# Moving the gathers, the inverse roots and two query/key products in a three-stream transformer kernel

## The chip, the cores and the metric

The kernel runs on one core of a Trainium2 chip. The metric is the device time of one launch, in microseconds (us). The engines are called as in the profile: PE (TensorE), DVE (VectorE), ACT (ScalarE), POOL (GpSimd) and SP (SyncE, which issues DMAs).

## The reference

For each of 32 batches of 224 rows of 512 columns, three residual layers follow one another, all in fp32:

```python
x = x + attn(layernorm(x))            # 16 heads of 32 columns, softmax over 224 keys, output product, bias
x = x + xattn(ctx, ctx, layernorm(x)) # one head of 512 columns over 750 context rows
x = x + ffn(layernorm(x))             # router scores over 2048 keys, top 8, softmax w,
                                      # agg = sum_k w_k * aux_values[top_idx_k]
# ffn(h) = h + gate * agg; gate = sigmoid(g1 * u + g0),
# u = clip(0.5 * log1p(var(h)) / mean over all rows of log1p(var(h)) + 2.5 * sigmoid(learned), 0, 5)
```

The gate of any row needs a mean over all rows of all batches, so the gathered sum `agg` of each batch is parked in DRAM and is scaled and added to the output at the very end.

## The kernel before

A batch is held as two tiles of 112 rows (`T` = 2). Its work is cut into steps that belong to streams: N (moments and scaling of the first layer's input), A (self-attention), R (residual load and bias), X (cross-attention), F (router, top 8, uncertainty), G (gather and weighted sum) and Z (the final scaling). One turn `i` of the loop in `pipeline` works on batch i+1 in N, i in A and R, i-1 in X, i-2 in F and i-3 in G. Turns 0 to 2 and 30 and 31 are unrolled, 3 to 29 are a hardware loop, and `LAST` lists what is left after turn 31. `ORDER` is the order of the steps in a turn, written out by hand. Each engine walks through the same list in order and carries out its part of each step, so a step's place in `ORDER` is its place in every engine's queue, and engines meet only by semaphores. `FIRST` and `SETUP` place the weight preparation.

**The attention heads** are done in four groups `k` of four heads. `("A","qk",k)` is the query and key product (24 matmuls, L1145); ACT copies its high part to `qk_hi` (L670) and DVE takes the rest, `qk_lo` (L897), which empties the PSUM bank. `("A","score",k)` is the head-score group, 24 small matmuls (L1211) into the four banks of `psA`; DVE takes the negated maxima `nmax` (L919), ACT exponentiates (L686), DVE normalises in `("A","share",k)` (L932, L934), PE transposes in `("A","prob",k)` (L1154) and ACT copies out (L642), PE mixes with the values in `("A","mix",k)` (L1234), ACT copies `oT_hi` (L703) and DVE takes `oT_lo` (L897). `psA` has four banks, handed out in turn by `FILL`; `scores` waits until all four are empty, among them the one that the step before filled, and the fourth transposed block of `("A","prob",k)` reuses the bank of the mix or product that stands right before it.

**Layer norms.** `statistics` (L828) on DVE: two `bn_stats`, two `bn_aggr`, `ve` = variance + 1e-5 (L840), then the inverse root by a bit-level first guess (L845) and three Newton rounds of three instructions on [112, 2] (L849 to L853), each waiting for the one before. `norm` (L856) then scales the tile. For stream F, `f_norm` does a second round of `bn_stats` and `bn_aggr` on the normed tile (L885, L890) and stores its variance to `var_all` (L893). For stream N the inverse roots go to DRAM (`store_moments`, SP) and come back spread over all partitions (`spread_moments`); DVE multiplies the transposed input with them in `("N","center")` (`centered`, L902).

**The gathers.** A batch needs 16 row gathers, in 8 chunks of two (`gather`, L584 to L593), into a buffer of two chunks, `vg`. POOL issues them as indirect DMAs. `first_gather` issues chunks 0 and 1 after the second top 8, and `next_gather` issues chunk c + 2 as soon as DVE has summed chunk c in `("G","sum",c)` (`g_sum`, L1007), whatever the other engines do at that time. POOL also issues the DMAs that add a bias (`bias_x`, `bias_x1`), adds `x2` and `xnf` in `add_base` (L582), and before any of these waits for eight small loads (`small_loaded`), which ACT issues.

**Around the end of a turn** the list reads `("A","prob",3)`, load, `("G","sum",7)`, `("F","score",3)`, `("F","top",1)`, `("A","mix",3)`, bias; the next turn begins with `("A","qk",0)`, `("A","qk",1)`, `("A","score",0)`.

## Time and profile before

| | |
|---|---|
| median of 3 runs | 2802.99 us (2800.82 to 2810.18) |
| profiled execution, its own time | 2808.96 us |
| its span | 2807.1 us, granted clock 0.971 of full |
| PE busy | 2570.2 us, 92% of the span |
| DVE busy | 2143.4 us, 76% |
| ACT busy | 1438.1 us, 51% |
| POOL busy | 682.9 us, 24% |
| DMA queues, share of 16 engines | 24.3% (issued by POOL) and 23.4% (by SP) |

The page cuts the span into 40 slices; these three lines show PE's busy tenths, DVE's, and the granted clock:

```profile
PE   6899999999999999999999999999999999999830
DVE  5446888888888888888888888888888888887552
PEclk9899999999999999999999999999999999999865
```

PE is busy nine tenths or more in 35 of the 40 slices; the first three and the last three are the preparation of the weights and the final scaling. "issue" as a releaser means that the profile shows nobody that was waited for; "remote" and "another core or an unknown queue" are the same for a wait whose other side has no record.

### The profile page before, as it was taken

The numbers are of one execution on the slowest core, as the hardware profiler recorded it, in microseconds if no ns is written. First come the engines' busy times: TensorE is split into PE (matmuls) and PEld (weight loads), VectorE is DVE, ScalarE is ACT, GpSimd is POOL, SyncE is SP. The second block draws the span as 40 slices with busy tenths as digits, with TensorE's granted clock in tenths as the row PEclk, the third lists the DMA queues.
The fourth block names the chain that finished last, engine by engine and source line by source line (L and its number), as shares of the span: only waits on it lengthen the run. The fifth ranks groups of instructions, "written<-read, shape, count | busy, mean of one in ns | idle before, by whom it ended". The sixth has DMA issues, their size and how long they took to land.

```text
span 2807.1 us, 56939 instructions
## 1 busy us (share of the span) xinstructions
PE 2570.2 (92%) x19090; PEld 2104.5 (75%) x19090; DVE 2143.4 (76%) x4207; ACT 1438.1 (51%) x4247; POOL 682.9 (24%) x650
## 2 busy tenths in 40 slices
PE   6899999999999999999999999999999999999830
PEld 4578878887788788877887888778878887788620
DVE  5446888888888888888888888888888888887552
ACT  2345555555555555555555555555555555555252
POOL 0001222222222222222222222222222222222244
PEclk9899999999999999999999999999999999999865
DMA  5223344454444454544444445444444444443799
GB/s 188 54 78 90 105 128 129 112 137 130 130 129 116 121 130 110 137 130 130 123 114 128 129 113 137 130 130 127 115 123 128 114 137 130 131 122 108 186 209 193
DMA packets 131544, 358.88 MB, mean 128 GB/s; under 512 B 21907, under 2 KB 26515, under 8 KB 123268
## 3 DMA queue, kind: packets, MB, share of 16 engines
q0 software_dynamic: 63520, 160.60, 24.3%
q1 hardware_dynamic: 63190, 192.16, 23.4%
q10 hardware_dynamic: 4784, 5.46, 0.6%
q8 instruction: 30, 0.49, 0.1%
q14 instruction: 20, 0.16, 0.0%
HBM read 316.38 MB, written 41.78 MB: 128 GB/s over the span
## 4 chain that ended last, share of the span: by engine, by line
PE 64%; issue 14%; DVE 10%; ACT 7%; DMA 2%; another core or an unknown queue 1%; POOL 1%; DVEq 0%; POOLq 0%; ACTq 0%; SPq 0%
PE psX L1145 26%; PE psA L1145 19%; PE psA L1211 5%; PE psF L1145 5%; PE psA L1154 4%; ACT pa L686 3%; PE psA L1234 2%; DVE nmax L919 2%; PE psX L1154 2%; DMA vg<-in_L_ffn_aux_values,idx 1%; DVE pa L934 1%; DVE top L1001 1%; DVE idx L1004 1%; ACT xT_hi L665 1%
## 5 line engine op out<-in xcount | busy, mean ns | idle before, releaser
L591 POOL DMA_INDIRECT vg<-in_L_ffn_aux_values,idx x512 | 492.4, 962 | 1585.2 <-DVE agg L1030 1066.8
L686 ACT ACTIVATE pa<-psA,nmax 112x224 f32<-112x224 f32 x1024 | 444.8, 451 | 246.2 <-DVE nmax L919 242.9
L919 DVE TENSOR_REDUCE nmax<-psA 112x4 f32<-112x896 f32 x256 | 267.3, 1086 | 137.1 <-PE psA L1211 125.5
L1145 PE MATMUL psX<-big,gT 128*112 128x375 f32 x1024 | 333.4, 478 | 0.6 <-ACT gT L713 0.6
L1030 DVE SCALAR_TENSOR_TENSOR agg<-vg,wt,agg 112x512 f32<-112x512 f32 x406 | 304.3, 749 | 9.2
L1145 PE MATMUL psX<-pT,cx 125*128 125x224 f32 x1536 | 299.1, 355 | 0.0
L1145 PEld LDWEIGHTS psX<-pT,cx 125*128 125x128 f32 x1536 | 288.0, 190 | 4.0 <-issue 0.3
L934 DVE TENSOR_TENSOR pa<-pa,rsum 112x896 f32<-112x896 f32 x256 | 279.5, 1092 | 8.8
L1145 PEld LDWEIGHTS psX<-big,gT 128*112 128x112 f32 x1024 | 175.2, 176 | 125.9 <-issue 0.9
L1154 PE MATMUL psA<-ident,pa 112*112 112x112 f32 x2048 | 240.6, 263 | 28.4 <-DVE oT_lo L897 24.6
L642 ACT COPY paT<-psA 112x448 f32<-112x448 f32 x512 | 243.3, 555 | 21.5 <-PE psA L1154 16.9
L1154 PEld LDWEIGHTS psA<-ident,pa 112*112 112x112 f32 x2048 | 202.1, 134 | 63.9 <-DVE oT_lo L897 38.1
L686 ACT ACTIVATION_READ_ACCUMULATOR pa<-psA,nmax 112x1 f32 x1024 | 212.1, 207 | 0.0
L1145 PE MATMUL psX<-xnxT,m 128*128 128x224 f32 x1024 | 201.8, 356 | 0.6 <-ACT xnxT L642 0.6
L1145 PEld LDWEIGHTS psX<-xnxT,m 128*128 128x128 f32 x1024 | 193.1, 192 | 1.4 <-ACT xnxT L642 1.0
L723 ACT ACTIVATE nx<-psX,xmax 112x375 f32<-112x375 f32 x128 | 72.4, 571 | 225.3 <-issue 161.0
L1001 DVE MAX8 top<-sc 112x8 f32<-112x2048 f32 x64 | 146.5, 2290 | 35.0 <-ACT sc L642 35.0
L1145 PE MATMUL psA<-xT_hi,wqT_hi 128*128 128x224 f32 x512 | 153.4, 300 | 5.9 <-DVE wkT_lo L1052 5.9
L642 ACT COPY sc<-psF 112x512 f32<-112x512 f32 x256 | 138.1, 594 | 19.2 <-PE psF L1145 17.4
L670 ACT CAST qk_hi<-psA 128x448 fp32r<-128x448 f32 x128 | 68.3, 533 | 154.0 <-PE psA L1145 154.0
L1004 DVE FIND_INDEX8 idx<-top,sc 112x8 uint32<-112x2048 f32 x64 | 146.3, 2286 | 0.0
L1145 PE MATMUL psA<-wvT_hi,xT_hi 128*112 128x256 f32 x512 | 143.7, 281 | 0.0
(220 smaller groups left out, 5952.9 us busy)
## 6 DMA issues: line engine op xcount, KB each, us to landing
big<-in_ctx_t SPq DMA_DIRECT2D x32, 1500.0 KB, 7.9
cx<-in_ctx SPq DMA_DIRECT2D x32, 1344.0 KB
xa<-in_x SPq DMA_DIRECT2D x64, 224.0 KB
centered<-in_x_t SPq DMA_DIRECT2D x32, 448.0 KB, 4.7
x<-in_L_attn_bff POOLq DMA_DIRECT2D x32, 448.0 KB, 6.2
x<-cb_scratch POOLq DMA_DIRECT2D x32, 448.0 KB, 5.9
x<-in_x SPq DMA_DIRECT2D x31, 448.0 KB
out<-x SPq DMA_DIRECT2D x30, 448.0 KB, 3.1
```

The costliest lines, as they stand in the source:

```text
L591: pool.indirect_dma_start(vg[:, c % SLOTS, k, :], None, aux_values, bass.IndirectOffsetOnAxis(ap=idx[:, t, n:n + 1], axis=0))\
L642: nc.scalar.copy(dst, src).then_inc(drained[s][j % banks[s]], 1)
L686: last = nc.scalar.activation(pa[:, t, h, :], psA[0:R, h, t * S:(t + 1) * S], ACT.Exp, bias=nmax[:, k % 2, h, t:t + 1], accum_out=rsum[:, ...
L723: nc.scalar.activation(px[:, t, j * HK:(j + 1) * HK], bank("X", job)[0:R, 0:HK], ACT.Exp, bias=xmax[:, t:t + 1], accum_out=xsum[:, t, j:j ...
L919: nc.vector.tensor_reduce(nmax[:, k % 2, h:h + 2, :], psA[0:R, h:h + 2, 0:T * S].rearrange("p h (t s) -> p h t s", t=T), AX_X, ALU.max, ne ...
L934: nc.vector.tensor_tensor(pa[:, t, :, :], pa[:, t, :, :], rsum[:, k, t, :].unsqueeze(2).to_broadcast([R, HB, S]), ALU.mult).then_inc(a_sha ...
L1001: mark("F", nc.vector.max(top[:, t, :], sc[0:R, :]))
L1004: nc.vector.max_index(idx[:, t, :], top[:, t, :], sc[0:R, :]).then_inc(sc_searched, 1)
L1030: last = nc.vector.scalar_tensor_tensor(dst, vg[:, c % SLOTS, k, :], w, dst, ALU.mult, ALU.add)
L1145: last = nc.tensor.matmul(dst, stationary, moving, start=n == 0, stop=n == len(pairs) - 1)
L1154: return nc.tensor.transpose(dst, src, ident[0:k, 0:k])
L1211: last = nc.tensor.matmul(psA[0:R, h, t * S:(t + 1) * S], qkT[q][own, k % 2, t * R:(t + 1) * R], qkT[key][own, k % 2, S:2 * S], start=n == ...
```

## The change

- `("G","sum",c)` no longer issues gathers. New steps `("G","gather",p)` and `("F","gather",0)` issue chunks 2p and 2p+1, four indirect DMAs in a row (`behind_scores`). In the loop POOL first waits until the head-score group before it in the list is complete. The sums of chunks 0 and 1 move into the turn before, as `("F","sum",0)` and `("F","sum",1)`, one on either side of `("A","mix",3)`.
- The inverse root of all three norms becomes one POOL instruction, `ve ** -0.5`, in new steps `("N"/"X"/"F","root",0)`. `statistics` keeps its first three steps and stands in a `"stat"` step of its own; for N it moves from behind `("A","score",1)` to behind `("A","score",0)`.
- The second statistics of stream F go. POOL computes variance times inverse root squared, by two instructions behind `add_base`, and stores them to `var_all`; ACT's final logarithm waits for that.
- `("A","qk",0)` and `("A","qk",1)` of batch i+1 become `("Q","qk",0)` and `("Q","qk",1)` in turn i, between `("A","prob",3)` and `("A","mix",3)`.
- `("F","score",3)` moves up between the two `("X","out")` steps, `("G","sum",7)` behind `("A","score",3)`, `("X","prob",0)` in front of `("A","mix",0)`, `("X","prob",1)` behind `("A","mix",1)`, and value and the third query/key product change places. `("X","enter")` becomes two steps, one for each tile. `LAST` is rewritten to match.

```diff
 ORDER = (
-    ("A", "qk", 0), ("A", "qk", 1), ("A", "score", 0), ("G", "sum", 0), ("A", "share", 0), ("X", "enter", 0),
-    ("X", "norm", 0), ("A", "value", 0), ("G", "sum", 1), ("A", "qk", 2), ("X", "turn", 0), ("A", "prob", 0),
-    ("F", "norm", 0), ("X", "query", 0), ("A", "score", 1), ("N", "norm", 0), ("F", "turn", 0), ("X", "score", 0),
-    ("N", "spread", 0), ("G", "sum", 2), ("G", "sum", 3), ("A", "qk", 3), ("A", "share", 1), ("X", "score", 1),
-    ("N", "center", 0), ("F", "route", 0), ("A", "mix", 0), ("X", "prob", 0), ("A", "prob", 1), ("F", "learn", 0),
-    ("X", "prob", 1), ("G", "sum", 4), ("F", "score", 0), ("A", "mix", 1), ("F", "score", 1), ("G", "sum", 5),
-    ("A", "score", 2), ("F", "top", 0), ("A", "share", 2), ("G", "sum", 6), ("X", "mix", 0), ("X", "mix", 1),
-    ("A", "prob", 2), ("F", "score", 2), ("A", "score", 3), ("X", "out", 0), ("A", "share", 3), ("X", "out", 1),
-    ("A", "mix", 2), ("A", "prob", 3), ("R", "load", 0), ("G", "sum", 7), ("F", "score", 3), ("F", "top", 1),
-    ("A", "mix", 3), ("R", "bias", 0),
+    ("A", "score", 0), ("N", "stat", 0), ("A", "share", 0), ("X", "enter", 0), ("X", "enter", 1), ("A", "qk", 2),
+    ("G", "gather", 1), ("N", "root", 0), ("X", "stat", 0), ("X", "root", 0), ("X", "norm", 0), ("A", "value", 0),
+    ("N", "spread", 0), ("X", "turn", 0), ("F", "stat", 0), ("G", "sum", 2), ("A", "prob", 0), ("F", "root", 0),
+    ("F", "norm", 0), ("X", "query", 0), ("G", "sum", 3), ("A", "score", 1), ("G", "gather", 2), ("F", "turn", 0),
+    ("A", "share", 1), ("X", "score", 0), ("A", "qk", 3), ("G", "sum", 4), ("X", "score", 1), ("N", "center", 0),
+    ("F", "route", 0), ("X", "prob", 0), ("A", "mix", 0), ("A", "prob", 1), ("F", "learn", 0), ("F", "score", 0),
+    ("G", "sum", 5), ("A", "mix", 1), ("X", "prob", 1), ("F", "score", 1), ("A", "score", 2), ("F", "top", 0),
+    ("G", "gather", 3), ("A", "share", 2), ("X", "mix", 0), ("X", "mix", 1), ("G", "sum", 6), ("A", "prob", 2),
+    ("F", "score", 2), ("A", "score", 3), ("G", "sum", 7), ("X", "out", 0), ("F", "score", 3), ("A", "share", 3),
+    ("X", "out", 1), ("A", "mix", 2), ("A", "prob", 3), ("F", "top", 1), ("F", "gather", 0), ("Q", "qk", 0),
+    ("R", "load", 0), ("F", "sum", 0), ("Q", "qk", 1), ("A", "mix", 3), ("R", "bias", 0), ("F", "sum", 1),
 )
...
-FIRST = (("N", "norm", 0), ("N", "spread", 0), ("W", "mean", 0), ("N", "center", 0), ("W", "split", 0),
+FIRST = (("N", "stat", 0), ("N", "root", 0), ("N", "spread", 0), ("W", "mean", 0), ("N", "center", 0), ("W", "split", 0),
          ("W", "mean", 1), ("W", "mean", 2), ("W", "split", 1), ("W", "split", 2), ("W", "keys", 0),
-         ("W", "keys", 1),)
+         ("W", "keys", 1), ("Q", "qk", 0), ("Q", "qk", 1), ("W", "keys", 2))
...
             def store_moments(b, _):
-                sp.wait_ge(steps["N"], N_STEPS * (b + 1))
+                sp.wait_ge(rooted["N"], b + 1)
...
                 nc.gpsimd.tensor_tensor(dst[:, :, :], x2[:, :, :], xnf[:, :, :], ALU.add).then_inc(base_ready, 1)
+                nc.gpsimd.tensor_tensor(var_part[:, :], mv["F"][:, :, 1], rstd["F"][:, :], ALU.mult).then_inc(var_step, 1)
+                pool.wait_ge(var_step, b + 1)
+                nc.gpsimd.tensor_tensor(columns(var_all, b), var_part[:, :], rstd["F"][:, :], ALU.mult).then_inc(var_taken, 1)
+
+            def norm_root(s):
+                def step(b, _):
+                    pool.wait_ge(steps[s], per_batch[s] * b + MOMENTS)
+                    if s == "N":
+                        wait(pool, moments_stored, 16 * b)
+                    apart(pool)
+                    nc.gpsimd.tensor_tensor(rstd[s][:, :], ve[s][:, :], power[:, :], ALU.pow).then_inc(rooted[s], 1)
+                return step
...
-            def next_gather(b, c):
-                if c + SLOTS < CHUNKS:
-                    gather(b, c + SLOTS)
-
-            def first_gather(b, t):
-                if t == 1:
-                    for c in range(SLOTS):
-                        gather(b, c)
+            def behind_scores(b, pair):
+
+                if not (isinstance(b, int) and b + 3 >= B + (pair == 0)):
+                    k = (pair - 1) % NB
+                    for h in range(HB):
+                        wait_full(pool, "A", head_job(k, h), b + 3 - (pair == 0))
+                for c in range(SLOTS * pair, SLOTS * pair + SLOTS):
+                    gather(b, c)
...
             def norm(s, b, src, dst, normed):
-                statistics(s, b, src, rstd[s][:, :])
+                dve.wait_ge(rooted[s], b + 1)
```

## Rows read from the trace of the kernel before

**Rows 1.** Windows: us, busy of PE, PEld, DVE, ACT, POOL (instructions), clock, DMA, GB/s

```profile
1000.00:2000.00 1000.00, 970.18 (x7394) 805.32 (x7393) 820.67 (x1629) 534.24 (x1611) 253.17 (x237) 1.00 0.46 125
```

**Rows 2.** Waits of PE, 1000 to 2000 us: engine, line, waited for: total, times, longest

```profile
PE psA L1211 <- issue: 18.6, 13, 1.4
...
PE psA L1154 <- DVE oT_lo L897: 8.4, 25, 0.4
```

**Rows 3.** PE timeline, two turns of the loop: start, us, line, out<-in [idle<-releaser]

```profile
1250.61 0.36 PE L1211 MATMUL psA<-qk_hi 32*112 32x224 f32 x4 [1.43 <-issue]
...
1265.39 0.93 PE L1154 MATMUL psX<-ident,nx 112*128 112x112 f32 x8
...
1294.71 0.59 PE L1154 MATMUL psA<-ident,pa 112*112 112x112 f32 x4 [0.39 <-DVE oT_lo L897]
...
1312.18 0.36 PE L1211 MATMUL psA<-qk_hi 32*112 32x224 f32 x4
...
1331.31 0.36 PE L1211 MATMUL psA<-qk_hi 32*112 32x224 f32 x4 [1.43 <-issue]
...
1392.85 0.36 PE L1211 MATMUL psA<-qk_hi 32*112 32x224 f32 x4
...
1411.31 0.36 PE L1211 MATMUL psA<-qk_hi 32*112 32x224 f32 x4 [1.43 <-issue]
```

**Rows 4.** DVE timeline, the same turns, columns as in PE's

```profile
1251.59 2.09 DVE L919 TENSOR_REDUCE nmax<-psA 112x4 f32<-112x896 f32 x2 [1.18 <-PE psA L1211]
...
1261.11 0.17 DVE L840 TENSOR_SCALAR ve_X<-mv_X 112x2 f32<-112x2 f32 x1
...
1294.27 0.39 DVE L897 TENSOR_TENSOR oT_lo<-psA,oT_hi 128x224 fp32r<-128x224 f32 x1
...
1314.64 2.09 DVE L919 TENSOR_REDUCE nmax<-psA 112x4 f32<-112x896 f32 x2 [1.91 <-remote]
...
1330.47 0.62 DVE L897 TENSOR_TENSOR qk_lo<-psA,qk_hi 128x448 fp32r<-128x448 f32 x1 [0.68 <-ACT qk_hi L670]
...
1394.65 2.09 DVE L919 TENSOR_REDUCE nmax<-psA 112x4 f32<-112x896 f32 x2 [1.25 <-PE psA L1211]
```

**Rows 5.** POOL timeline, the gathers beside head-score group 3, columns as in PE's

```profile
1313.73 0.92 POOL L591 DMA_INDIRECT vg<-in_L_ffn_aux_values,idx  x1 [0.30 <-issue]
...
1394.40 0.93 POOL L591 DMA_INDIRECT vg<-in_L_ffn_aux_values,idx  x1 [0.30 <-issue]
```

**Rows 6.** Waits of all engines, whole run, columns as in PE's waits

```profile
DVE nmax L919 <- remote: 11.6, 6, 1.9
```

**Rows 7.** Groups by line on DVE: out<-in xcount | busy us, mean ns | idle

```profile
L1030 DVE SCALAR_TENSOR_TENSOR agg<-vg,wt,agg 112x512 f32<-112x512 f32 x406 | 304.3, 749 | 9.2
...
L849 DVE SCALAR_TENSOR_TENSOR tmp_X<-rstd_X,ve_X 112x2 f32<-112x2 f32 x96 | 15.5, 161 | 4.1 <-DVE rstd_X L853 0.3
```

**Rows 8.** ACT timeline, around the first mix and the loop's end, columns as in PE's

```profile
1293.82 0.34 ACT L703 CAST oT_hi<-psA 128x224 fp32r<-128x224 f32 x1
...
1294.05 0.45 ACT L642 COPY pT<-psX 125x336 f32<-125x336 f32 x1
...
1329.91 0.53 ACT L670 CAST qk_hi<-psA 128x448 fp32r<-128x448 f32 x1 [2.03 <-PE psA L1145]
```

**Rows 9.** Groups by line on POOL, columns as in those of DVE

```profile
L582 POOL TENSOR_TENSOR x<-x,nx 112x1024 f32<-112x1024 f32 x31 | 73.0, 2355 | 93.5 <-DVE nx L859 93.5
```

**Rows 10.** DVE timeline, first 90 us: the first batch's scaled input

```profile
25.72 1.09 DVE L902 TENSOR_TENSOR centered<-centered,spread 128x896 f32<-128x896 f32 x1 [12.69 <-DMA spread<-moments_scratch]
```

**Rows 11.** ACT timeline, first 90 us: the last of the eight small loads

```profile
23.48 0.45 ACTq L619 DMA_DIRECT2D gbc<-in_L_ffn_gate_bias  x1
```

**Rows 12.** DMA issues, first 60 us: queue, size, us to landing

```profile
gbc<-in_L_ffn_gate_bias ACTq DMA_DIRECT2D x1, 0.4 KB, 3.7
```

**Rows 13.** PE timeline, end of the first batch's head mix

```profile
92.94 1.00 PE L1154 MATMUL psA<-ident,pa 112*112 112x112 f32 x4 [3.67 <-DVE oT_lo L897]
```

**Rows 14.** Windows, first batch, columns as in the first group

```profile
90.00:100.00 10.00, 5.31 (x46) 3.14 (x47) 5.06 (x9) 3.86 (x8) 0.00 (x0) 0.60 0.44 155
```

More of the change, by code:

```diff
@@ L28 @@
 F32R = mybir.dt.float32r
-I32 = mybir.dt.int32
 U32 = mybir.dt.uint32
@@ L231, in build @@
         rstd = {s: sb(f"rstd_{s}", [R, T]) for s in "NXF"}
-        tmp = {s: sb(f"tmp_{s}", [R, T]) for s in "NXF"}
+        power = sb("power", [R, T])
+        var_part = sb("var_part", [R, T])
         var_all = sb("var_all", [R, B * T])
@@ L540, in _ @@
                           ("W", "cb"): first_cxT, ("W", "gb"): first_ctx,
-                          ("X", "score"): next_cxT, ("X", "mix"): next_ctx, ("N", "norm"): store_moments,
+                          ("X", "score"): next_cxT, ("X", "mix"): next_ctx, ("N", "root"): store_moments,
                           ("N", "spread"): spread_moments, ("N", "center"): next_xt, ("X", "enter"): entered, ("R", "load"): next_xr,
                           ("F", "norm"): store_base,
-                          ("G", "sum"): store_agg})
+                          ("G", "sum"): store_agg, ("F", "sum"): store_agg})
             for k in range(LATE + B - DIRECT):
@@ L558, in _ @@
             nc.gpsimd.memset(one[:, :], 1.0)
+            nc.gpsimd.memset(power[:, :], -0.5).then_inc(const_step, 1)
+            pool.wait_ge(const_step, 2)
             nc.gpsimd.memset(rwT[:, RD:LO], 0.0)
@@ L612, in _ @@
             pool.wait_ge(small_loaded, 16 * SMALL)
-            pipeline(pool, {("Z", "scale"): add_scaled,  ("R", "bias"): bias_x, ("X", "norm"): bias_x1, ("F", "norm"): add_base,
-                            ("G", "sum"): next_gather, ("F", "top"): first_gather})
+            pipeline(pool, {("Z", "scale"): add_scaled,  ("R", "bias"): bias_x, ("N", "root"): norm_root("N"), ("X", "root"): norm_root("X"), ("F", "root"): norm_root("F"), ("X", "norm"): bias_x1, ("F", "norm"): add_base,
+                            ("G", "gather"): behind_scores, ("F", "gather"): behind_scores})
         @block.scalar
@@ L835, in statistics @@
                 apart(dve)
+                if s == "F":
+                    wait(dve, var_taken, b)
+                    apart(dve)
                 for t in range(T):
@@ L937, in share, with x_enter @@
                 assert k < NB - 1 or count["A"] == A_STEPS
[L939 to L945 removed]
+            def x_enter(b, t):
+                if t == 0:
+                    dve.wait_ge(xr_biased, 16 * (b + 1))
+                j = FILL["X", "enter", t]
+                wait_full(dve, "X", j, b)
+                nc.vector.tensor_tensor(x1[:, t, :], bank("X", j)[0:R, :], x1[:, t, :], ALU.add)\
+                    .then_inc(drained["X"][j % banks["X"]], 1)
             def x_maxima(b, t):
```

102 lines of the change are left out of this document (39 added, 63 removed), and 68 rows, old and new, of tables (LAST, SETUP).

## The prediction

> **What bounds the kernel now.** I read the windows first: between 1000 and 2000 us PE is busy 970.18 of 1000 us at full granted clock, DVE 820.67 [rows 1]. So PE bounds the loop, and an edit pays there only as far as it takes away one of PE's gaps, about 2.4 us in a turn of 80. The waits of PE name them [rows 2]: 18.6 us in 13 waits in front of a head-score group, 8.4 us in 25 in front of the fourth transposed block of a `prob` step. The PE timeline places them [rows 3]. The first is 1.43 us, in front of head-score group 0 at 1250.61, 1331.31 and 1411.31: PE has run out of work and waits for the second query/key product to be copied by ACT and DVE. The blocks cost 0.39 us at 1294.71 (head group 1) and, by what is left of the 8.4 us over 12.4 turns, 0.29 us in head group 3. The turns are not equal: 1250.61 to 1331.31 is 80.70 us, 1331.31 to 1411.31 is 80.00. From head-score group 3 to the next turn's group 0 they take 19.13 us (1312.18 to 1331.31) and 18.46 us (1392.85 to 1411.31), so the whole difference arises there.
>
> **Why there:** the maxima on DVE. Behind head-score group 0 they begin 0.98 us after the group (1250.61, 1251.59). Behind group 3 they begin after 1.80 us (1392.85, 1394.65) or after 2.46 us (1312.18, 1314.64), and DVE sits idle meanwhile, 1.25 or 1.91 us [rows 3, 4]. POOL is issuing gathers at that moment: the second of a pair begins at 1394.40, 0.25 us before the maxima of the quicker turn; in the slower one it begins at 1313.73 and ends at 1314.65, when the maxima begin [rows 5]. I read this as: a gather that is being issued while a head-score group ends holds back the news of that end by 0.8 or 1.5 us. The longer delay is the "remote" wait, 6 in the whole run [rows 6], so I take 6 turns in 28 for slow ones, 0.22.
>
> **The change, part by part,** first a turn of the loop.
>
> *Gathers behind a head-score group.* POOL now waits until the group is complete, as DVE does, and four gathers take about 5 us, so none is running when the next group ends. The maxima of group 3 then come at 0.98. Behind them the chain of DVE from the maxima to `qk_lo` took 16.45 us in the slow turn (1314.64 to 1331.09 [rows 4]). It loses some 2 us of waiting and gains the chunk sum that now stands in front of the second `qk_lo`, two instructions and two small ones, some 1.9 us at 0.75 an instruction [rows 7]. So it ends near 0.98 + 16.4 = 17.4 us, and PE is the later one:
>
> *Query/key products moved back.* The wait of 1.43 us does not vanish, it changes its object: group 0 needs all four banks, and `("A","mix",3)` now fills the last of them, directly in front of it. In place of `qk_hi` (0.53) and `qk_lo` (0.62) the wait covers `oT_hi` (0.34) and `oT_lo` (0.39) [rows 4, 8]: 1.43 - 0.19 - 0.23 = 1.01 us. Queued behind it is all of PE. With `("F","score",3)` moved up as cover, the 0.29 us of head group 3 go too. Head-score group 3 to the next group 0: 18.46 - 1.43 - 0.29 + 1.01 = 17.75 us. That is 0.71 less in a normal turn and 1.38 less in a slow one, 0.78 x 0.71 + 0.22 x 1.38 = 0.86 us in the mean.
>
> *X prob 0 in front of mix 0.* ACT now copies `pT` before `oT_hi`. In the trace `oT_hi` stands at 1293.82, `oT_lo` at 1294.27, the block at 1294.71 [rows 3, 4, 8]. `oT_hi` moves to about 1294.15 and `oT_lo` behind DVE's own copy of that step, to about 1294.70, so the block waits till 1295.14. PE's work up to it is the same, hence 0.43 us more of waiting. X prob 1 behind mix 1 covers later banks that had no wait; nothing.
>
> *Roots on POOL.* Per turn DVE loses 27 Newton instructions at 161 ns [rows 7], three first guesses and the second statistics, some 7 us. PE never waits for these in the loop, so this is worth nothing there. What counts is the way back. X norm waits for POOL, and behind it in DVE's queue stand X norm, F stat and the sums; PE's X turn waits for it. Before, `ve_X` is ready 10.67 us and X turn due 14.78 us after group 0 [rows 3, 4]. After, N stat (1.9) stands in front, the Newton rounds are gone, both enters and the third `qk_lo` come first; I add DVE's queue up to `ve_X` at 12.3 us. The norm takes 1.0, so a root may take 14.8 - 13.3 = 1.4 us from `ve_X` to DVE's next start. The trace has no small two-input instruction on POOL. Upper end: the [112, 1024] addition, 2.36 us [rows 9], and 0.7 of signalling, 3.1 us. Lower end: 0.3, signalling alone. I take 0.7, near the lower end, since a root has 2 columns and the addition 1024. That hides. N root has 25 us until it is needed, F root has a chunk sum beside it, and SP's spread of the moments comes earlier.
>
> The Trainium skill (GPSIMD Engine Reference, 3.1) gives 4497 ns for an addition of 2048 columns; with the 2355 ns of this trace for 1024 [rows 9] that leaves an estimate of 0.2 us for two. By it the root takes about 0.5 us, and the sum stays.
>
> A turn: -0.86 + 0.43 = -0.43 us; 28 turns: **-12 us**. Bounds: -1.0 (the 0.43 doesn't come) to +0.3 a turn (the delay isn't the gathers').
>
> *Start.* DVE had the first root ready at 13.0 us and then waited 12.69 us for its store and spread, while the weights were loading; the input is scaled at 25.72 [rows 10]. Now the root is POOL's, and POOL waits for eight small loads before its first step. The last is issued at 23.48 and lands 3.7 us later, at 27.2 [rows 11, 12]; the root comes near 27.8, and store and spread follow. With the queues emptier I take 7.7 us, so the input is scaled at 35.5: **+9.8 us** (7 to 14), and nothing hides it, since the splits of the weights stand behind it in DVE's queue.
>
> *First turns.* The second batch's moments come 25 us earlier, so the spread is there when DVE asks. PE's wait of 3.67 us [rows 13] goes, and with it most of the half clock behind it (0.60 granted from 90 to 100 us, that is, near 1.2 GHz [rows 14]): **-7 us** (-3.7 to -9). Turns 1 and 2 have the same gaps and some more at `prob` and `mix`: **-2 us**.
>
> *Tail.* Before X turn of the last batch DVE drops nine Newton instructions and a first guess (about 2 us with their gaps), and a chunk sum leaves from in front of it (1.3), against 0.7 for the root and, later, 0.5 for the variance behind `add_base`: **-2.2 us** (-8 to +6), if the scaling that follows starts so much earlier.
>
> Sum: 9.8 - 7 - 2 - 12 - 2.2 = **-13.4 us**. The profiled execution took 2808.96 us, 1.9 more than its span, and becomes 2795.6. It lies 6 us above the median, so on the median: 2802.99 - 13.4 = **2789.6 us**.
>
> **The rivals.**
> *Late root (slower).* If POOL needs more than 1.4 us for the way `ve_X`, root, DVE, PE waits for X turn in each of 30 turns. For: a power is no addition, and no row prices it. Against: two columns only. At 2.2 us: 0.8 x 30 = 24 us, 2813.6; at the upper end of 3.1: +51, 2841. It outweighs the gain from 1.4 + 13.4/30 = 1.85 us on. Chance 0.13.
> The skill's same page (2.1) says that the first call of freshly loaded POOL code costs about 6 us; paid once, in the start, where the first root is on the path, it would give 2795.6, and no row here shows it.
> *Late gathers (slower).* Chunk 0 is now issued behind group 3 and summed in front of the second `qk_lo` and of `oT_lo`, both of which PE waits for. It has some 7 us to land, beside the context load, as the chunks of group 3 had before, when DVE did not wait. Decides from 7 us on; 1 us late is +28, 2818. Chance 0.07.
> *The delay is not the gathers'* or follows them to where they now run (mix 2). The 0.6 to 0.9 us of the loop stay, the 0.43 comes: 2789.6 + 12 = 2802. For: two clock readings side by side are no cause. Chance 0.22.
> *No growth at the first mix,* so -25 us, 2777.6. Chance 0.08.
>
> **How the numbers follow.** Forecast 0.50 (2781 to 2797). The range takes in "no growth" and most of the late rivals: 2773 to 2814. A measurement of this kernel tells 0.3%, 8.4 us, from no change. Faster by more (below 2794.6): 0.46 of the forecast's 0.50, the 0.08 of the last rival and 0.04 of the third, together 0.58. Within: the other 0.04 of the forecast and 0.18 of the third, 0.22. Slower (above 2811.4): the first two rivals, 0.20.
>
> **What the profile after would show.** The maxima of groups 2 and 3 begin 1.0 us after their group; no "remote" waits. Group 3 to group 0 takes 17.75 us, with a wait of 1.0 in front of group 0 that `oT_lo` ends. The block at mix 0 waits 0.8. X turn has no wait, and the root lasts below 1 us. The first scaled input stands near 35.5. DVE's busy time falls by some 220 us. A wait at X turn, or of DVE for `vg`, would make the prediction wrong.

## The result, and the profile after

| | before | after |
|---|---|---|
| median, us | 2804.19 (2800.82 to 2810.18, 4 runs) | 2768.00 (2767.13 to 2768.09, 4 runs) |
| ratio, 95% interval | | 0.9873 [0.9857, 0.9889] |
| profiled execution, us (its span) | 2808.96 (2807.1) | 2767.93 (2766.1) |
| DVE busy, us | 2143.4 | 1976.6 |
| turn of the loop, mean of 28, us | 80.19 | 79.11 |

The changed kernel is faster by 36 us, 1.3%. I had forecast 13 (2789.6, range 2773 to 2814): the sign is right, the size is not.

The start of head-score group 0 in turns 1, 3 and 31 cuts the 41.0 us by which the spans of the two profiled executions differ into stages (before's execution lies 4.8 us above the median of its four, so the medians differ by 36.2 only). With the forecast beside them:

| stage | before | after | difference | forecast |
|---|---|---|---|---|
| to group 0 of turn 1 | 132.06 | 129.93 | -2.1 | +2.8 |
| turns 1 and 2 | 156.03 | 155.86 | -0.2 | -2 |
| turns 3 to 30 | 2245.42 | 2215.06 | **-30.4** | -12 |
| from there to the end | 273.59 | 265.25 | -8.3 | -2.2 |

The page of after, its first part: busy time, share, instructions.

```profile
PE 2549.4 (92%) x19090; PEld 2107.2 (76%) x19090; DVE 1976.6 (71%) x3087; ACT 1442.4 (52%) x4247; POOL 862.9 (31%) x811
```

The window that answers to [rows 1], columns as there:

```profile
1000.00:2000.00 1000.00, 976.54 (x7468) 816.60 (x7467) 763.63 (x1197) 549.52 (x1645) 330.44 (x305) 1.00 0.48 126
```

PE is still the bound and idles 1.9 us a turn in place of 2.4. Its waits over the whole run (those of [rows 2] are of one stretch), columns as there:

```profile
PE psA L1216 <- DVE oT_lo L902: 32.7, 31, 1.1
PE psA L1159 <- DVE oT_lo L902: 24.9, 30, 0.9
```

One turn of its timeline, columns as in [rows 3]:

```profile
1314.24 0.36 PE L1216 MATMUL psA<-qk_hi 32*112 32x224 f32 x4 [1.05 <-DVE oT_lo L902]
...
1328.92 0.93 PE L1159 MATMUL psX<-ident,nx 112*128 112x112 f32 x8
...
1358.63 0.59 PE L1159 MATMUL psA<-ident,pa 112*112 112x112 f32 x4 [0.82 <-DVE oT_lo L902]
...
1363.19 0.36 PE L1216 MATMUL psA<-qk_hi 32*112 32x224 f32 x4
...
1375.75 0.36 PE L1216 MATMUL psA<-qk_hi 32*112 32x224 f32 x4
...
1393.37 0.36 PE L1216 MATMUL psA<-qk_hi 32*112 32x224 f32 x4 [1.10 <-DVE oT_lo L902]
```

The wait before group 0 is 1.05 to 1.10 us and ended by `oT_lo` (forecast 1.01; it was 1.43 [rows 3]). The block at the first mix waits 0.82 (forecast 0.8). X turn at 1328.92 has no wait. DVE's timeline of the same turn:

```profile
1326.36 0.17 DVE L863 TENSOR_SCALAR ve_X<-mv_X 112x2 f32<-112x2 f32 x1
1327.51 1.00 DVE L869 TENSOR_SCALAR nx<-x,mv_X,rstd_X 112x512 f32<-112x512 f32 x2 [0.98 <-POOL rstd_X L603]
...
1332.89 3.51 DVE L1035 SCALAR_TENSOR_TENSOR agg<-vg,wt,agg 112x512 f32<-112x512 f32 x2
...
1364.19 1.09 DVE L924 TENSOR_REDUCE nmax<-psA 112x4 f32<-112x896 f32 x1 [1.31 <-PE psA L1216]
...
1376.75 1.09 DVE L924 TENSOR_REDUCE nmax<-psA 112x4 f32<-112x896 f32 x1 [0.73 <-PE psA L1216]
```

POOL's:

```profile
1326.71 0.69 POOL L603 TENSOR_TENSOR rstd_X<-ve_X,power 112x2 f32<-112x2 f32 x1 [4.33 <-DVE ve_X L863]
...
1333.06 2.80 POOL L592 TENSOR_TENSOR x<-x,nx 112x1024 f32<-112x1024 f32 x1 [1.22 <-DVE nx L869]
...
1365.22 0.92 POOL L613 DMA_INDIRECT vg<-in_L_ffn_aux_values,idx  x1 [19.78 <-issue]
...
1377.84 0.92 POOL L613 DMA_INDIRECT vg<-in_L_ffn_aux_values,idx  x1 [8.01 <-issue]
```

The gathers now begin 2.0 and 2.1 us after groups 2 and 3 (1363.19, 1375.75), the maxima 1.00 us after them, where they came after 1.8 and 2.5 at group 3 [rows 3, 4]. No "remote" wait is left and no turn is longer than the others: the turns take 79.08 to 79.16 us, the last 79.30. The root lasts 0.69 us.

### The profile page after: what moved, and what is told of

The parts are those of the page before. It is cut to its first block, busy times and chain, and to the rows that moved or that the text cites. A ratio compares the mean times of both kernels' runs of the same rounds, so it can differ in the third digit from the quotient of the medians.

```text
span 2766.1 us, 55689 instructions
## 1 busy us (share of the span) xinstructions
PE 2549.4 (92%) x19090; PEld 2107.2 (76%) x19090; DVE 1976.6 (71%) x3087; ACT 1442.4 (52%) x4247; POOL 862.9 (31%) x811
## 4 chain that ended last, share of the span: by engine, by line
PE 78%; DVE 8%; ACT 5%; issue 4%; DMA 2%; POOL 1%; ACTq 1%; DVEq 0%; POOLq 0%
PE psX L1150 41%; PE psA L1150 17%; PE psA L1159 6%; PE psF L1150 5%; PE psA L1216 4%; PE psA L1239 3%; PE psX L1159 2%; ACT L769 1%; DMA vg<-in_L_ffn_aux_values,idx 1%; DVE xmax L955 1%; PE psF L1159 1%; DVE top L1006 1%; ACT xT_hi L687 1%; DVE oT_lo L902 1%; DVE idx L1009 1%
## 5 line engine op out<-in xcount | busy, mean ns | idle before, releaser
L613 POOL DMA_INDIRECT vg<-in_L_ffn_aux_values,idx x512 | 542.8, 1060 | 1208.1 <-issue 1071.3
L1035 DVE SCALAR_TENSOR_TENSOR agg<-vg,wt,agg 112x512 f32<-112x512 f32 x406 | 361.6, 891 | 10.7
L1159 PE MATMUL psA<-ident,pa 112*112 112x112 f32 x2048 | 229.4, 263 | 24.9 <-DVE oT_lo L902 24.9
L1159 PEld LDWEIGHTS psA<-ident,pa 112*112 112x112 f32 x2048 | 202.0, 134 | 57.2 <-DVE oT_lo L902 31.5
L664 ACT COPY paT<-psA 112x448 f32<-112x448 f32 x512 | 237.6, 553 | 14.9 <-PE psA L1159 14.6
L902 DVE TENSOR_TENSOR qk_lo<-psA,qk_hi 128x448 fp32r<-128x448 f32 x128 | 79.2, 619 | 112.5 <-ACT qk_hi L692 112.3
```

Of the source, the lines that this page charges most:

```text
L613: pool.indirect_dma_start(vg[:, c % SLOTS, k, :], None, aux_values, bass.IndirectOffsetOnAxis(ap=idx[:, t, n:n + 1], axis=0))\
L664: nc.scalar.copy(dst, src).then_inc(drained[s][j % banks[s]], 1)
L902: return nc.vector.tensor_tensor(dst, src, hi.bitcast(F32), ALU.subtract)
L1035: last = nc.vector.scalar_tensor_tensor(dst, vg[:, c % SLOTS, k, :], w, dst, ALU.mult, ALU.add)
L1159: return nc.tensor.transpose(dst, src, ident[0:k, 0:k])
```

## Experiments

All kernels of a series ran on one chip (the first two series on the same one), each compared with the kernel before beside it. Group starts below are from PE's timelines, "lag" is the time from a head-score group's start to its maxima on DVE. Mean spacing of the groups over turns 3 to 30, us:

| kernel | group 0 to 1 | 1 to 2 | 2 to 3 | 3 to 0 | turn |
|---|---|---|---|---|---|
| before | 23.25 | 25.44 | 12.88 | 18.61 | 80.19 |
| e1, before with gathers behind groups 2, 3 | 23.23 | 25.46 | 12.56 | 18.01 | 79.27 |
| after | 23.16 | 25.81 | 12.56 | 17.58 | 79.11 |
| e2, after, gathers free | 23.52 | 26.80 | 13.33 | 17.59 | 81.25 |
| e3, after, X prob 0 behind mix 0 | 23.19 | 25.41 | 12.56 | 17.58 | 78.74 |
| e5, before with a clock on ACT; no lags | 23.27 | 25.43 | 12.56 | 17.99 | 79.26 |
| e6, after, Newton on DVE | 25.30 | 25.80 | 12.57 | 17.60 | 81.27 |
| e7, after, qk 0 and 1 in their own turn | 23.23 | 25.81 | 12.57 | 18.88 | 80.49 |
| e8, after, F score 3 behind prob 3 | 25.05 | 25.81 | 12.57 | 19.63 | 83.05 |
| e12, after, root twice | 23.71 | 25.81 | 12.56 | 17.58 | 79.66 |
| e15, e2's kernel again; no lags | 23.17 | 25.80 | 12.57 | 17.59 | 79.13 |

**First series: the gathers, the swap, the first root.** The kernel before took 2805.05 us (2799.11 to 2806.99, 7 runs).

e1 is the kernel before with GpSimd waiting until group 2 or 3 is complete (`behind`); no step moves:

```diff
             def next_gather(b, c):
+                if c == 4:
+                    behind(2, b + 3)
...
                 if t == 1:
+                    behind(3, b + 2)
                     for c in range(SLOTS):
```

> The kernel before, with one edit: GpSimd waits for head-score group 2 before it issues the four gathers that ran beside it, and for group 3 before the first two of the next pair. Nothing else moves. Theory (a gather issued while a group ends holds the maxima back, and late maxima of group 2 are also what makes PE wait inside the third prob step): the maxima of groups 2 and 3 begin 1.0 us after their group, no turn is longer than the others, group 2 to group 3 falls from 12.86 to 12.56 us; a turn falls from 80.19 in the mean to 79.7, the time by 10 to 14 us, ratio 0.995. My prediction's own step knew only the slow turns here: 4 us. Rival (the delay is not the gathers', it comes from the sums on DVE): lags stay 1.7 to 1.8, ratio 1.000.

Measured 2777.89 us, ratio 0.9905 [0.9889, 0.9922]: 27 us, twice what even the better theory gave, and three quarters of the whole change. A turn loses 0.92 us in two places. The first is the third `prob` step. In before, on PE, and then DVE's second `share`:

```profile
1389.98 2.02 PE L1154 MATMUL psA<-ident,pa 112*112 112x112 f32 x16
1391.77 0.46 PE L1145 MATMUL psF<-rk,rq_hi 113*112 113x512 f32 x1
```

On DVE:

```profile
1389.80 1.09 DVE L934 TENSOR_TENSOR pa<-pa,rsum 112x896 f32<-112x896 f32 x1
```

The same steps in e1, on PE, and on DVE also the maxima of group 3, which stands at 1378.27 there (lag 1.01):

```profile
1375.70 1.70 PE L1162 MATMUL psA<-ident,pa 112*112 112x112 f32 x16
1377.17 0.47 PE L1153 MATMUL psF<-rk,rq_hi 113*112 113x512 f32 x1
```

On DVE:

```profile
1374.89 1.09 DVE L942 TENSOR_TENSOR pa<-pa,rsum 112x896 f32<-112x896 f32 x1
...
1379.28 1.09 DVE L927 TENSOR_REDUCE nmax<-psA 112x4 f32<-112x896 f32 x1 [0.78 <-PE psA L1219]
```

Sixteen transposed blocks take 1.79 us up to the next step in before and 1.47 in e1. The timeline groups them in one row, so no wait is printed, but the second `share` ends at 1390.89 in before, when eight of the blocks (0.75 us) are through and the other eight need it; in e1 it ends at 1375.98, 0.28 us after the step began. That is 0.32 us a turn, from group 2's maxima. The other place is the fourth `prob` step, on PE in before:

```profile
1401.91 0.59 PE L1154 MATMUL psA<-ident,pa 112*112 112x112 f32 x4 [0.26 <-DVE oT_lo L897]
1402.28 0.46 PE L1145 MATMUL psF<-rk,rq_hi 113*112 113x512 f32 x1
```

And in e1:

```profile
1385.74 1.75 PE L1162 MATMUL psA<-ident,pa 112*112 112x112 f32 x16
1387.25 0.46 PE L1153 MATMUL psF<-rk,rq_hi 113*112 113x512 f32 x1
```

The step began at 1400.30 in before: 1.98 us against 1.51 in e1, with no step moved. The `oT_lo` it waits for stood in DVE's queue behind the late maxima. With the turns of 0.67 us more, group 3 to group 0 loses 0.60 in the mean.

e2 takes the waits out of the changed kernel:

```diff
             def behind_scores(b, pair):
-                if not (isinstance(b, int) and b + 3 >= B + (pair == 0)):
-                    k = (pair - 1) % NB
-                    for h in range(HB):
-                        wait_full(pool, "A", head_job(k, h), b + 3 - (pair == 0))
                 for c in range(SLOTS * pair, SLOTS * pair + SLOTS):
```

> The changed kernel without the waits for the head-score groups in front of the fours; the gathers keep their place in GpSimd's order and go as soon as their slots are free, so by the sums' times some run at about 23, 48 and 61 us of a turn, where groups 1, 2 and 3 end. Theory: maxima lag by 1.5 to 1.9 us where a gather is beside the end of a group, the third prob step again takes 1.7 to 1.8 us in place of 1.47, a turn grows from 79.11 by 0.3 to 0.6 us: ratio to the kernel before 0.990 to 0.994, +8 to +17 us on the changed kernel. Rival (the gain has nothing to do with the gathers): 0.987 as the changed kernel.

Measured 2831.88 us, ratio 1.0093 [1.0076, 1.0110]: 64 us more than the changed kernel. Lags of 1.9 or 2.6, 2.4 and 2.2 us at groups 0, 1 and 2; at group 3, where no gather is beside, 1.0. The direction is as expected, the size four times the upper end.

e3 puts `("X", "prob", 0)` behind `("A", "mix", 0)` again:

```diff
-    ("F", "route", 0), ("X", "prob", 0), ("A", "mix", 0), ("A", "prob", 1),
+    ("F", "route", 0), ("A", "mix", 0), ("X", "prob", 0), ("A", "prob", 1),
```

> The changed kernel with X prob 0 put behind A mix 0 again, as before the change. Theory (ACT's pT copy ahead of oT_hi costs PE 0.43 us in each turn): the wait in front of the fourth block of head group 1 falls from 0.82 to 0.4 us, group 1 to group 2 from 25.80 to 25.4, a turn from 79.11 to 78.7, the time by 11 to 12 us to about 2756: ratio 0.983. Rival (what PE gains there it waits for at the next X step or at head-score group 2): a turn stays 79.1, ratio 0.987.

Measured 2755.95 us, ratio 0.9829 [0.9813, 0.9846]: 12 us. A row of PE's waits shows it; it was 24.9 in 30:

```profile
PE psA L1159 <- DVE oT_lo L902: 12.2, 31, 0.7
```

e4 moves one line:

```diff
                     nc.gpsimd.tensor_tensor(rstd[s][:, :], ve[s][:, :], power[:, :], ALU.pow).then_inc(rooted[s], 1)
+                    if s == "N" and isinstance(b, int) and b == 0:
+                        pool.wait_ge(small_loaded, 16 * SMALL)
...
-            pool.wait_ge(small_loaded, 16 * SMALL)
             pipeline(pool, {
```

> The changed kernel with GpSimd's wait for the eight small loads moved behind its first root. Theory (that wait alone delayed the first scaled input): root at 10.8 instead of 24.3 us, its store and spread under the weight loads as before the change, first scaled input near 25 us instead of 33.1, score group 0 near 48.5 instead of 56.1, the time 7 to 8 us shorter, near 2760: ratio 0.9845. Rival (the load queues set it, and what is gained is waited for at the weights or at the first turn's set-up work): 0 to 3 us, ratio 0.987.

Measured 2765.46 us (2760.08 to 2766.94), ratio 0.9864 [0.9848, 0.9880]. On POOL and on DVE:

```profile
11.26 0.73 POOL L603 TENSOR_TENSOR rstd_N<-ve_N,power 112x2 f32<-112x2 f32 x1 [8.84 <-DVE ve_N L864]
```

On DVE:

```profile
26.30 1.09 DVE L908 TENSOR_TENSOR centered<-centered,spread 128x896 f32<-128x896 f32 x1 [15.23 <-DMA spread<-moments_scratch]
```

The same steps in the changed kernel, on POOL:

```profile
24.30 0.73 POOL L603 TENSOR_TENSOR rstd_N<-ve_N,power 112x2 f32<-112x2 f32 x1 [21.89 <-DMA gbc<-in_L_ffn_gate_bias]
```

On DVE:

```profile
33.09 1.09 DVE L907 TENSOR_TENSOR centered<-centered,spread 128x896 f32<-128x896 f32 x1 [22.29 <-DMA spread<-moments_scratch]
```

The root comes 13.0 us earlier, the scaled input 6.8: store and spread take 14.3 us beside the weight loads and 8.1 behind them. In the profiled execution group 0 of turn 1 stands 6.3 us earlier and the end 7.9; the median of four gains 2.5. The mechanism is as expected, its worth varies between executions.

**Second series: what the other edits are worth.** Here the kernel before took 2777.18 us (2775.09 to 2778.87, 7 runs), 28 less than before. e5 shows why: it is the kernel before with a clock on ACT.

```diff
+                if k == 3:
+                    wait_full(act, "A", head_job(k, 3), b)
+                    nc.scalar.copy(probe[:, :], one[:, :])
```

> The kernel before; ACT also waits for head 3 of head-score group 3 and copies one column of a constant then, as a clock of when the news of the group reaches another engine (in that place ACT is idle for 2.2 us). If PE's signal itself is held up by a gather, the copy stands 1.7 to 1.8 us after the group, as the maxima do. If only DVE is held up, the copy stands at 1.0 us or less and the maxima still at 1.8. No change in time, 2800 to 2810 us.

Measured 2779.72 us, in one execution. ACT, DVE and POOL around group 3 at 1376.88:

```profile
1377.93 0.19 ACT L685 COPY probe<-one 112x1 f32<-112x1 f32 x1 [0.18 <-PE psA L1215]
```

On DVE:

```profile
1377.88 2.09 DVE L923 TENSOR_REDUCE nmax<-psA 112x4 f32<-112x896 f32 x2 [0.74 <-PE psA L1215]
```

On POOL:

```profile
1376.91 0.92 POOL L592 DMA_INDIRECT vg<-in_L_ffn_aux_values,idx  x1 [7.66 <-DVE agg L1034]
```

A gather runs from 0.03 to 0.95 us after the group, and the maxima come at 1.00. At group 2 the gather runs from 0.27 to 1.24 us and the maxima come at 1.15; in the profiled execution of before it ran from 0.26 to 1.25 there, and they came at 1.74. A turn takes 79.26 us: that of e1, 79.27, and each of the four spacings is e1's within 0.04 us. So in this series gathers beside a group's end cost nothing, and late maxima cost the kernel before the same 0.9 us a turn whether their absence comes by e1's edit or by itself. The copy on ACT, 1.05 us behind the group's start (the texts of e13 and e17 put it at 0.8), could not say which engine is late, since none was.

e6 takes all three roots back to DVE, Newton's rounds as before the change, in the new order:

```diff
                 mark(s, nc.vector.tensor_scalar(ve[s][:, :], mv[s][:, :, 1], EPS, None, ALU.add))
+                mark(s, nc.vector.tensor_scalar(root.bitcast(I32), ve[s][:, :].bitcast(I32), -0.5, RSQRT_SEED,
+                                                ALU.mult, ALU.add))
+                for _ in range(3):
...
             def norm(s, b, src, dst, normed):
-                dve.wait_ge(rooted[s], b + 1)
```

> The changed kernel with all three roots back on DVE by Newton's rounds, in the new order of steps. Theory: N's and X's rounds (2.1 us each) stand in DVE's queue before nx, GpSimd's way of 1.15 us goes; nx begins 2 to 3 us later than 13.27 us into the turn, PE waits 1.5 to 2.5 us for X turn in each turn, +40 to +70 us; the start gains back the 7.4 us, the tail loses 3 to 4: 2800 to 2835 us, ratio 1.000 to 1.011. Rival (DVE's queue has room, the roots are worth nothing in the loop as my prediction said): no wait at X turn, the time about 2764, ratio 0.986.

Measured 2827.56 us, 60 above the changed kernel's 2768. PE and DVE:

```profile
1355.95 0.51 PE L1175 MATMUL psX<-ident,nx 112*128 112x112 f32 x3 [1.70 <-DVE nx L885]
```

On DVE:

```profile
1354.81 1.00 DVE L885 TENSOR_SCALAR nx<-x,mv_X,rstd_X 112x512 f32<-112x512 f32 x2 [0.15 <-DVE rstd_X L880]
```

`nx` begins 15.46 us into the turn in place of 13.27, and X turn 16.60 in place of 14.68. In three of the 28 turns group 0 to 1 takes 26.98 us in place of 25.11; in the first of them the granted clock is 0.60 from 381.24 to 384.24 us, behind PE's wait for `nx`. In the old order the same rounds cost PE nothing [rows 3]; in the new one GpSimd's roots are what makes room.

e7 puts the two products back at the head of their turn, and takes them out of the steps ahead of the loop:

```diff
-    ("A", "score", 0), ("N", "stat", 0),
+    ("A", "qk", 0), ("A", "qk", 1), ("A", "score", 0), ("N", "stat", 0),
...
-    ("F", "gather", 0), ("Q", "qk", 0), ("R", "load", 0), ("F", "sum", 0), ("Q", "qk", 1), ("A", "mix", 3),
+    ("F", "gather", 0), ("R", "load", 0), ("F", "sum", 0), ("A", "mix", 3),
...
-         ("W", "keys", 1), ("Q", "qk", 0), ("Q", "qk", 1), ("W", "keys", 2))
+         ("W", "keys", 1), ("W", "keys", 2))
```

> The changed kernel with the first two query/key products back at the head of the next turn. Theory: the wait in front of group 0 covers qk_hi and qk_lo again, 1.43 in place of 1.05 to 1.10 us: +0.35 a turn, +10 to +12 us, ratio 0.991. Rival (the wait is set by the sum in front of qk_lo on DVE, whatever the order): no change, 0.987, or more than 1 us a turn.

Measured 2831.47 us. Group 3 to group 0 grows by 1.30 us, not 0.35: prob 3 and mix 3 now stand directly behind one another (PE waits 0.77 for `paT`), and the wait before group 0 is 1.47. Another 23 us are lost before turn 1 (152.67 against 129.93). `SETUP` counts the A steps of the first turn, so with two more of them at its head every later piece of weight preparation also comes two A steps earlier; how the 23 us divide between that and the products is not shown. The rival's "more than 1 us a turn" is nearer than the theory.

e8 puts F score 3 back:

```diff
-    ("X", "out", 0), ("F", "score", 3), ("A", "share", 3), ("X", "out", 1), ("A", "mix", 2), ("A", "prob", 3), ("F", "top", 1),
+    ("X", "out", 0), ("A", "share", 3), ("X", "out", 1), ("A", "mix", 2), ("A", "prob", 3), ("F", "score", 3), ("F", "top", 1),
```

> The changed kernel with F score 3 back behind prob 3. By my prediction's step (it is only cover for one block): the block waits 0.3 us again, +8 us, ratio 0.990. Theory now: DVE's search for the top eight follows it by 2.1 us, and behind the search stand both qk_lo, a sum and oT_lo, so group 0 starts about 2.2 us later in each turn: +60 us, ratio 1.008 to 1.010, with a wait of some 3 us in front of group 0 that oT_lo ends.

Measured 2885.20 us: 117 above the changed kernel, of which group 3 to 0 gives 2.05 us a turn, close to the 2.2, and group 0 to 1 another 1.9 that nobody expected. PE and DVE:

```profile
1451.88 0.53 PE L1216 MATMUL psA<-qk_hi 32*112 32x224 f32 x4 [2.65 <-DVE oT_lo L902]
```

On DVE:

```profile
1443.77 2.29 DVE L1006 MAX8 top<-sc 112x8 f32<-112x2048 f32 x1 [2.37 <-ACT sc L664]
```

The search begins at 74.45 us of its turn in place of 70.75. The 1.9 us are no wait: `nx` is late in the turn, but PE does not wait at X turn. They are TensorE's clock. PE has idled 2.65 us in front of group 0, and the window behind it, columns as in [rows 1], has a granted clock of 0.50, that is, near 1.2 GHz:

```profile
1451.80:1456.30 4.50, 4.42 (x31) 3.50 (x32) 4.20 (x6) 1.70 (x7) 1.40 (x2) 0.50 0.01 2
```

The same stretch of the changed kernel, behind a wait of 1.10 us:

```profile
1393.30:1397.80 4.50, 4.43 (x40) 3.52 (x41) 4.46 (x6) 2.06 (x9) 1.97 (x2) 1.00 0.54 91
```

Some of the matmuls behind group 0 take 0.63 us in place of 0.40, in all 28 turns. So of the 117 us some 57 are the later search (28 times 2.05) and some 53 come through the clock (28 times 1.89).

**Third series: both together, and the changed kernel once more.** The kernel before took 2804.38 us (2802.31 to 2809.11, 7 runs). e9 has the edits of e3 and e4, shown there:

> The changed kernel with both edits that paid alone: X prob 0 behind A mix 0 (12 us) and GpSimd's wait for the small loads behind its first root (2.5 to 8 us). They lie in different stages and add: 2748 to 2754 us. Its gathers stand behind the head-score groups, so the time should be the same whether the kernel before takes 2805 us (ratio 0.981) or 2777 us (0.991) beside it.

Measured 2747.18 us (2744.76 to 2749.49), ratio 0.9794 [0.9777, 0.9810]. This version beats both kernels.

e10 is the changed kernel with no edit:

> The changed kernel, unchanged, timed beside the kernel before once more, since the kernel before took 2805 us in the first series and 2777 in the second, without any late maxima in the second. Theory (the delay by gathers is a property of where or when the kernel runs; the changed kernel has no gather beside the end of a group and so never shows it): the changed kernel takes 2766 to 2770 us either way; ratio 0.987 if the kernel before takes 2805, 0.997 if it takes 2777. Rival (everything gets faster by 1 percent in the second series): 2740 us beside 2777, ratio 0.987.

Measured 2768.66 us, ratio 0.9873 [0.9856, 0.9889], as the first time. It was never timed in a series without lags; e6, e7 and e8 are set against 2768 from elsewhere, but the spacings that they leave alone are the changed kernel's within 0.07 us (table).

e11 is e2's kernel, with e2's edit:

> The changed kernel without the waits in front of the fours, as in e2 (there 2832 us, 64 us above the changed kernel, with lags of 1.6 to 2.6 us at groups 0, 1 and 2). Theory: where the kernel before takes 2777 us a gather beside the end of a group delays nothing; lags 1.0 to 1.2, the time within 6 us of the changed kernel. Where the kernel before takes 2805 it is again near 2832.

Measured 2829.04 us, ratio 1.0089 [1.0071, 1.0107], with e2's lags, and 60 us above e10 beside it.

e12 computes each root twice:

```diff
+                    nc.gpsimd.tensor_tensor(spare_root[s][:, :], ve[s][:, :], power[:, :], ALU.pow).then_inc(root_step[s], 1)
+                    pool.wait_ge(root_step[s], b + 1)
                     nc.gpsimd.tensor_tensor(rstd[s][:, :], ve[s][:, :], power[:, :], ALU.pow).then_inc(rooted[s], 1)
```

> The changed kernel with each root on GpSimd computed twice, one after the other, the first into a spare tile. The way from ve_X to nx grows from 1.15 by 0.7 to 0.9 us. X turn is due 14.68 us into the turn and nx ends at 14.27; by Newton on DVE nx came 2.19 later and X turn 1.92, so the slack is 0.27 us: PE waits 0.45 to 0.6 us for X turn in each turn, +13 to +18 us: 2781 to 2786. By my prediction's limit (1.4 us from the end of ve_X, measured 0.98): +0.3 to 0.5 a turn, +8 to +14.

Measured 2786.61 us (2783.19 to 2790.71), 18 above the changed kernel.

```profile
1338.88 0.79 PE L1163 MATMUL psX<-ident,nx 112*128 112x112 f32 x6 [0.32 <-DVE nx L873]
```

On DVE:

```profile
1337.74 1.00 DVE L873 TENSOR_SCALAR nx<-x,mv_X,rstd_X 112x512 f32<-112x512 f32 x2 [1.74 <-POOL rstd_X L607]
```

`ve_X` to `nx` takes 1.91 us in place of 1.15, and a turn 0.55 more. So 0.2 us of 0.76 were slack.

**Fourth to sixth series: the lag itself.** The kernel before took 2778.66, 2778.03 and 2779.36 us here. None of the traces of e13 to e18 shows a lag, so all but e15 answer nothing they were made for.

> The changed kernel without the waits in front of the fours. Beside a kernel before at 2804 us: 2829 to 2832 as twice measured. Beside one at 2777 us: lags of 1.0 to 1.2 us with gathers beside the ends of groups 0, 1 and 2, and 2766 to 2775 us.

e15, e2's kernel a third time, measured 2769.47 us (2765.77 to 2771.52), ratio 0.9965 [0.9953, 0.9977]: the time of the changed kernel, and 60 us less than twice before. The same group 1 in e11, on PE:

```profile
1363.50 0.36 PE L1212 MATMUL psA<-qk_hi 32*112 32x224 f32 x4
```

On POOL:

```profile
1363.73 1.05 POOL L613 DMA_INDIRECT vg<-in_L_ffn_aux_values,idx  x1 [0.75 <-issue]
```

On DVE:

```profile
1365.93 1.09 DVE L920 TENSOR_REDUCE nmax<-psA 112x4 f32<-112x896 f32 x1 [3.38 <-PE psA L1212]
```

And in e15, on PE:

```profile
1340.04 0.36 PE L1212 MATMUL psA<-qk_hi 32*112 32x224 f32 x4
```

On POOL:

```profile
1340.23 1.05 POOL L613 DMA_INDIRECT vg<-in_L_ffn_aux_values,idx  x1 [0.75 <-issue]
```

On DVE:

```profile
1341.05 2.09 DVE L920 TENSOR_REDUCE nmax<-psA 112x4 f32<-112x896 f32 x2 [2.00 <-PE psA L1212]
```

The gather lies at 0.23 to 1.28 us behind the group in one, at 0.19 to 1.24 in the other; the maxima come at 2.43 and at 1.01. Set beside each other, the two traces differ, in the median, in no other wait of DVE or ACT for PE: `xmax`, for one, starts 0.58 us after the start of its last matmul in both.

> As e5: the kernel before with ACT's one-column copy when head 3 of head-score group 3 is done. Where the kernel before takes 2804 us: if PE's signal is late, the copy stands at 1.7 us or more behind the group (2.4 in the slow turns); if only DVE is held up, at 0.8 to 1.0 with the maxima at 1.8 to 2.5. Where it takes 2777 us: 0.8 us as in e5, and the maxima at 1.0.

e14 is e1 without its wait for group 3:

```diff
                 if t == 1:
-                    behind(3, b + 2)
                     for c in range(SLOTS):
```

> The kernel before with the four gathers beside group 2 moved behind that group, and nothing done at group 3. Theory: late maxima of group 2 cost PE 0.31 us inside the third prob step; group 2 to group 3 falls from 12.86 to 12.56, group 3 to group 0 stays 18.46 (19.13 in slow turns): -8 to -9 us, ratio 0.997, of e1's 27; the other 17 to 18 are group 3's. By my prediction's step group 2 costs nothing: 1.000. Where the kernel before takes 2777 us: no change.

e13 (e5's kernel) measured ratio 0.9996 [0.9985, 1.0006] and e14 0.9998 [0.9989, 1.0008], both with the lags of e5. The same two kernels were run again, e14's twice:

> The kernel of e14 (the kernel before with the gathers beside group 2 moved behind it, those beside group 3 left). Beside a kernel before at 2804 us: group 2 to group 3 falls from 12.86 to 12.56 us, group 3 to group 0 stays 18.46 or 19.13; -8 to -9 us, ratio 0.997. Beside one at 2778: no change, as e14.

> The kernel of e5 (ACT copies one column when head 3 of group 3 is done). Beside a kernel before at 2804 us: the copy at 1.7 us or more behind the group if PE's signal is late, at 0.8 to 1.0 us if only DVE is held up, the maxima at 1.8 to 2.5 in both cases. Beside one at 2778: 0.8 and 1.0 as in e5 and e13.

> The kernel of e14 once more, alone with the kernel before. Beside a kernel before at 2804 us: group 2 to group 3 12.56 us in place of 12.86, group 3 to group 0 unchanged at 18.46 or 19.13, -8 to -9 us, ratio 0.997. By my prediction's step, which charged group 3 alone: 1.000. Beside one at 2778: no change.

Ratios 1.0006 [0.9996, 1.0015], 0.9997 [0.9987, 1.0008] and 0.9998 [0.9989, 1.0007]. The kernel before has two times, 2804 with late maxima and 2778 without. It kept one of them through all runs of a series, and one chip showed both in two series. What sets it is open. So is whether PE's signal or DVE is late. The price of all late maxima, 0.9 us a turn, is shown twice, by e1 and by the kernel before without lags (e5, e13, e17); how it divides between those of group 2 and those of group 3 is read from the rows of e1 and before, and no run separates them.

## Why the prediction was wrong, step by step

**The mechanism was the right one.** A gather being issued while a head-score group ends holds the maxima back. e1 removes the overlap and moves no step, the lags go and 27 us with them; e2 and e11 bring it back to the changed kernel, the lags stand at the three groups that have a gather beside them and not at the fourth, and 60 to 64 us come. The rival "the delay is not the gathers'" is out. What the reading of two clock columns could not show is that the overlap is not enough: e5 and e15 have it without a lag.

**The term that was mis-sized is the price of a late maximum in the loop.** I charged it to the place where PE waits next for the end of DVE's chain, group 3 to group 0, and only in the slow turns: 0.22 x 0.67, some 0.15 us of the 0.86. It also costs 0.32 us in the third `prob` step, behind group 2, and 0.47 in the fourth, in all turns; e1 shows 0.92 us a turn, 26 in 28 turns. The late maxima of group 2 stood in my own text as a check and not in the sum. I had looked for waits printed in PE's rows. A wait inside a row "x16" isn't printed; the 1.79 us for sixteen blocks against 1.47 was there to be read. The 0.29 us that I put down to F score 3 as cover belong here too: in e1, where F score 3 stands in its old place, the block does not wait. Its move is worth something else, an earlier start of the search for the top eight (e8), which my sum did not have.

**The rest of the loop.** From e1 to after a turn loses 0.16 us: 0.43 between groups 3 and 0, of which 0.38 is the wait before group 0 (1.43 to 1.05, forecast 0.42 less), 0.07 between 0 and 1, against 0.35 more at mix 0 (forecast 0.43; e3 takes it back, 12 us as forecast). Group 3 to group 0 is 17.58 us, forecast 17.75.

**Roots.** Forecast way 0.7, limit 1.4 (14.8 - 13.3 is 1.5, so the line was worked out wrong as well), measured 0.98 us from the end of `ve_X` to `nx`; no wait. The limit was too generous: e12 lengthens the way by 0.76 and PE loses 0.55, so it is near 1.2. "Worth nothing in the loop" was wrong as a statement on the new order: without the roots on POOL it costs 60 us (e6). From the figure of the Trainium skill (GPSIMD Engine Reference, 3.1) I had estimated 0.2 us for the instruction and 0.5 for the way. The multiplication of the same size that writes `var_all` fits (0.20 us), but the root takes 0.69 and its way 0.98, so the estimate was too low for a power. The 6 us that the Trainium skill (GPSIMD Engine Reference, 2.1) gives for the first call of freshly loaded code do not show: the first root starts 0.2 us after the small load it waits for has landed (24.1, 24.30) and takes 0.73 us, and the rival at 2795.6 is out. *Late root* and *late gathers* did not come: no wait at X turn, and DVE has no wait for `vg` in the loop.

**Start.** Forecast +9.8, 7 to 14: the scaled input came 7.4 us later (25.72, 33.09), because the last small load landed at 24.1, not 27.2, with store and spread taking 8.1 us, assumed 7.7. The path was right; e4 shows it. The first turn gave back 9.3 (83.16 to 73.84 us), forecast 7, with full granted clock where it was 0.60 [rows 14]:

```profile
90.00:100.00 10.00, 8.12 (x46) 4.17 (x45) 3.67 (x6) 2.69 (x7) 0.00 (x0) 1.00 0.42 154
```

Turns 1 and 2 gained 0.2, not 2.

**Tail.** Forecast -2.2, measured -8.3. X turn of the last batch comes 3.6 us earlier behind group 0 of turn 31, and so does the gate (2692.26 - 2533.51 = 158.75, now 155.16):

```profile
2591.53 0.82 PE L1159 MATMUL psX<-ident,nx 112*128 112x112 f32 x3 [4.80 <-DVE nx L869]
...
2656.01 0.54 PE L1150 MATMUL psA<-one,gT 112*112 112x1 f32 x2 [10.63 <-DVE gT L1101]
```

That is 1.4 us above my term. With the roots back on DVE (e6) the gate stands at 158.02, so they are 2.9 of it; without the lags (e1) it stands at 157.85, 0.9 earlier than before. The other 4.8 come behind the gate, where DVE waits for `vg` 31.5 us in six waits, 38.3 in nine before. They belong neither to the roots nor to the lags: from the gate to the end before takes 114.9 us, e1 114.9, e6 110.3 and after 110.1. That gathers issued in fours land earlier there was only argued; no run isolates it.

Where the kernel before shows no lags it takes 2777 to 2779 us, and the changed kernel, by e15, which differs from it in waits that do nothing there, 2769: some 9 us, 0.35% (interval [0.9953, 0.9977]), a quarter of the 36. My 13.4 stands near that, but it was made from a trace with lags and held to one.

## What to carry to other kernels

When a producer is late, follow it to every consumer, and compare the time a grouped row takes with the same step where its operands are early: a wait inside the group has no mark. An edit that moves a step within a tuned order is worth what the rest of the order leaves it: X prob 0's move cost 12 us; taking F score 3's back cost 117, nearly half of it in matmuls slowed by a lower clock behind PE's longer wait. Look at the granted clock before you put a stretch that grew down to a wait. A gain seen against one series of runs may be that series' condition; time the kernel before beside each, and more than once.
